# Projections and self attention of a two-layer transformer kernel, joined in one program for each engine

## The chip, the cores and the metric

One core of a Trainium2 chip. The engines are TensorE (PE; PEld is its weight load), VectorE (DVE), ScalarE (ACT), GpSimd (POOL) and SyncE (SP), which here only issues DMAs. The metric is the device time of one execution in microseconds.

## The reference, cut to what matters

Two layers over x of shape (4, 1024, 256), each cross attention and then a feed-forward part. The change is in the first layer's feed-forward part, which begins with a self attention of 16 heads of 16:

```
src = layernorm(x)
q = (src @ q_w).reshape(b, s, h, hd).transpose(0, 2, 1, 3)
k = (src @ k_w).reshape(b, s, h, hd).transpose(0, 2, 1, 3)
v = (src @ v_w).reshape(b, s, h, hd).transpose(0, 2, 1, 3)
scores = jnp.einsum('bhqd,bhkd->bhqk', q, k) / np.float32(np.sqrt(hd))
scale = jax.nn.sigmoid(jnp.einsum('bhsd,hd->bhs', q, scale_w)) * 2.0
aw = jax.nn.softmax(scores * scale[..., None], axis=-1)
out = jnp.einsum('bhqk,bhkd->bhqd', aw, v).transpose(0, 2, 1, 3).reshape(b, s, d)
```

## The kernel before

`self_projections` runs over 8 chunks of 512 tokens (a batch is two chunks). For a chunk c, DVE normalizes x (`layernorm`, `ln_apply`), PE transposes the result and ACT copies it to `srcT`; PE then computes v (`vps`, L817), q (`qps`, L825) and k (`kps`, L832), transposes the next chunk (L807), and multiplies q by the scale weights (`zps`, L841). q and k are split into three bf16 parts each: ACT makes the first (`kpart[..., 0]`), DVE the rest (`krest`, L706), ACT the second part (L781), POOL the third (L736). For q, ACT's tanh of `zps` (`th`, L787) and a product on DVE (`qT`, L710) come first, then the same steps (L791, L715, L793, L740). SP stores all parts to DRAM (`q_parts`, `k_parts`, `v_groups`). The middle batches are a hardware loop. At the end SP waits for the last store, the block ends on all engines, and semaphores are cleared.

`self_attention` is a second block. It takes 16 groups of 4 heads, each loaded from DRAM into one of three sets of `qs`, `ks`, `vs`. A unit is a group and one half (512) of its queries; there are 32 units. A unit has 8 key tiles of 128. Scores are made transposed (keys on partitions), so the maximum over keys has to be known before: it is taken one or two units ahead from another product. A pair of matmuls (`first_scores`, L1106, in a buffer of `aps`) gives 128 queries by 512 keys of two heads, and DVE reduces it (`maximum`, L1020); a unit needs 16 of these pairs. `combine` joins them, PE transposes the maxima (`transpose_max`, L1118), ACT negates them (`keep_max`, L1064), POOL splits them (`split_max`) and SP passes them through DRAM (`pass_max`) into two rows of `qs`. In the main loop, every key tile has four `scores` (L1137) in three rotating buffers `bps`, one for each head, whose exponentials ACT writes to `ex` (L1086), and one `weigh_values` (8 matmul records, L1147) into `ops`. Two of the pairs for units ahead stand in each key tile. The order on PE is: a score, two pairs, a score, the weighing of the key tile before, two scores. The weighing waits for that tile's last exponential. Once in a unit ACT copies `ops` out (`keep_out`, L1056) and PE transposes it (L1127).

Before the main loop the 16 pairs of unit 0 and the first 12 of unit 1 are made with nothing beside them.

Of the kernel before, what the change touches and what calls it, by code (L numbers as in the profile page):

```python
# [13 lines left out]
P = 128  # L14
# [573 lines left out]
def self_projections(nc, x_sb, src_sb, ident, eps_pow, w, q_parts, k_parts, v_dram):  # L588

    with ExitStack() as ctx:  # L590
        kit = Kit(nc, ctx, "sp_")
        sb, ps, sem = kit.sb, kit.ps, kit.sem
        turnstile = sem("turnstile")
        wts = sb("wts", [P, 3, HALVES, D])
        swcol = sb("swcol", [P, HALVES])
        swblk = sb("swblk", [P, HALVES, P])
        stats, mv = sb("stats", [P, CT, 6]), sb("mv", [P, CT, 2])
        var, rstd = sb("var", [P, CT]), sb("rstd", [P, CT])
        xn = sb("xn", [P, CT, D])
# [2070 lines left out]
```

## Time and profile before

| | us |
|---|---|
| median of three runs | 2056.4 (2055.46 to 2056.41) |
| the profiled execution's own time | 2058.98 |
| its span, first to last instruction | 2056.9 |
| SP's first DMA of the projections | 248.9 |
| DVE's first statistics of the projections | 254.4 |
| first transpose, first v projection on PE | 259.2, 262.3 |
| first pair for the maxima | 392.4 |
| first exponential | 425.1 |
| last exponential | 1124.8 |

The stage in question is the stretch from 248 to 1133 us; what comes ahead and behind is not touched by the diff. In a timeline row, the first number is the start, the second the time until the end of the last of the merged instructions, and the brackets name what ended the idle time before it.

### The profile page before, as it was taken

To read this page: it belongs to the slowest core of one execution; us is meant where nothing else is said; L and a number is where in the kernel's file an instruction comes from. 1 tells how busy PE (TensorE), PEld (TensorE's weight loads), DVE (VectorE), ACT (ScalarE), POOL (GpSimd) and SP (SyncE) were. 2 spreads that over 40 slices of the span, in tenths; PEclk is the share of its full clock that TensorE was granted. 3 is DMA by queue.
4 is the path that set the end of the run, shared out by engine and by line. 5 is a ranking of instruction groups with operands and counts; after the bars stand their busy time and mean duration, and the time that the engine had idled before them with its cause. 6 is when DMAs were issued, how large, how long until landed. Compare 5 with 4: busy or idle time off the path is not lost. (4 is left out here: it accounts for less than half of the span.)

```text
span 2056.9 us, 30275 instructions
## 1 busy us (share of the span) xinstructions
PE 1713.4 (83%) x10579; PEld 808.6 (39%) x10580; DVE 1250.0 (61%) x2123; ACT 969.1 (47%) x1811; POOL 603.5 (29%) x645
## 2 busy tenths in 40 slices
PE   5799799389999999999997884999077996329997
PEld 3466455012222222222221563776044663125654
DVE  5344344588888888888881484665783554562221
ACT  3422256158888888888887331444242332102110
POOL 4300034613222122121122264666561001120533
PEclk9899989679999999999999995999588998758998
DMA  5000048711221111321100622221400003310542
GB/s 138 1 2 1 16 156 288 208 38 38 55 56 38 38 38 38 67 45 37 38 2 1 220 80 85 59 69 56 125 1 1 1 1 124 135 32 11 124 122 31
DMA packets 112675, 134.48 MB, mean 65 GB/s; under 512 B 18481, under 2 KB 88497, under 8 KB 112273
## 3 DMA queue, kind: packets, MB, share of 16 engines
q1 hardware_dynamic: 101824, 114.20, 20.5%
q0 software_dynamic: 9552, 17.83, 3.6%
q8 instruction: 86, 1.41, 0.3%
q10 hardware_dynamic: 1152, 0.54, 0.1%
q14 instruction: 61, 0.49, 0.1%
HBM read 78.47 MB, written 53.93 MB: 64 GB/s over the span
## 5 line engine op out<-in xcount | busy, mean ns | idle before, releaser
L1020 DVE TENSOR_REDUCE sa_mhalf<-sa_a 128x2 f32<-128x1024 f32 x512 | 602.3, 1221 | 86.8 <-PE sa_a L1106 86.8
L1086 ACT ACTIVATE sa_e<-sa_b 128x512 f32<-128x512 f32 x1024 | 534.5, 601 | 139.4 <-PE sa_b L1137 139.4
L1137 PE MATMUL sa_b<-sa_q,sa_k 112*128 112x512 bf16 x1024 | 311.1, 385 | 3.2 <-ACT sa_e L1086 3.0
L1147 PE MATMUL sa_ops<-sa_e,sa_v 128*17 128x512 f32 x2048 | 270.4, 599 | 6.3 <-ACT sa_e L1086 1.1
L1137 PEld LDWEIGHTS sa_b<-sa_q,sa_k 112*128 112x128 bf16 x1024 | 78.8, 97 | 322.6 <-ACT sa_e L1086 281.6
L1106 PE MATMUL sa_a<-sa_k,sa_q 48*128 48x512 bf16 x1024 | 168.2, 398 | 38.4 <-DMA sa_k<-k_parts 24.5
L993 POOL TENSOR_TENSOR sa_rden<-sa_o_rows,sa_minus_one 128x16 f32<-128x16 f32 x32 | 93.1, 2908 | 180.1 <-ACT sa_o_rows L1072 180.1
L213 DVE TENSOR_REDUCE xa_mx<-xa_rows 128x16 f32<-128x1024 f32 x64 | 78.3, 1224 | 102.6 <-PE xa_rows L445 102.6
L982 POOL CAST sa_negm<-sa_neg 16x128 bf16<-16x128 f32 x32 | 9.0, 281 | 380.1 <-issue 338.0
L1106 PEld LDWEIGHTS sa_a<-sa_k,sa_q 48*128 48x128 bf16 x1024 | 42.1, 93 | 177.6 <-issue 77.0
L360 ACT ACTIVATE xa_pT<-xa_cols 128x1024 f32<-128x1024 f32 x64 | 62.1, 1021 | 84.9 <-PE xa_cols L477 84.9
L2552 DVE TENSOR_TENSOR sw_hT<-sw_p,sw_act 128x512 f32<-128x512 f32 x32 | 22.1, 692 | 101.9 <-PE sw_p L2497 101.9
L2465 POOL DMA_INDIRECT out_x<-sw_yo,tc_idx x32 | 49.9, 1560 | 105.5 <-DVE sw_yo L2559 98.5
L1637 PE MATMUL ex_hps<-at_w,ex_xT 128*128 x156 | 77.3, 619 | 1.9 <-ACT ex_xT L1677 1.9
L445 PE MATMUL xa_rows<-xa_kblk,xa_qT 64*128 64x256 f32 x512 | 73.1, 407 | 6.1 <-DVE xa_mx L213 5.3
L2541 ACT ACTIVATE sw_act<-sw_p 128x512 f32<-128x512 f32 x32 | 19.1, 597 | 118.8 <-PE sw_p L2491 110.3
L1660 PE MATMUL ex_yps<-at_attn,ex_hT 128*128 x312 | 74.1, 380 | 0.5 <-ACT ex_hT L1687 0.4
L544 PE MATMUL xa_cols<-c_ctxT,c_wts 128*128 128x256 f32 x16 | 7.5, 652 | 78.0 <-PEq L43 64.5
L1687 ACT ACTIVATE ex_hT<-ex_tps,at_bt,at_g 128x128 f32<-128x128 f32 x156 | 58.8, 457 | 15.7 <-PE ex_tps L1648 15.7
L726 POOL TENSOR_TENSOR sp_var<-sp_mv,x_eps_pow 128x4 f32<-128x4 f32 x8 | 7.5, 939 | 190.7 <-DVE sp_mv L683 190.7
L2491 PE MATMUL sw_p<-sw_xT,tc_w 128*128 128x512 f32 x128 | 62.0, 608 | 1.2 <-ACT sw_xT L2530 1.2
L1147 PEld LDWEIGHTS sa_ops<-sa_e,sa_v 128*17 128x17 f32 x2048 | 34.9, 95 | 69.5 <-ACT sa_e L1086 48.8
(328 smaller groups left out, 2819.7 us busy)
## 6 DMA issues: line engine op xcount, KB each, us to landing
k_parts<-sp_kpart SPq DMA_DIRECT2D x96, 128.0 KB, 1.8
sa_q<-q_parts SPq DMA_DIRECT2D x64, 192.0 KB, 5.1
sa_k<-k_parts SPq DMA_DIRECT2D x64, 192.0 KB, 5.6
tc_w<-in_L_ffn_W SPq DMA_DIRECT2D x24, 512.0 KB
q_parts<-sp_qpart SPq DMA_DIRECT2D x16, 384.0 KB, 3.3
ex_xg<-expert_in SPq DMA_DIRECT2D x39, 132.0 KB
v_groups<-sp_vt SPq DMA_DIRECT2D x8, 544.0 KB, 4.1
sa_v<-v_groups SPq DMA_DIRECT2D x16, 272.0 KB, 7.3
```

The lines of the kernel that those rows point to most:

```text
L213: nc.vector.tensor_reduce(mx[:, t], rows[:].rearrange("p r (n k) -> p (r n) k", k=SC), axis=X, op=ALU.max).then_inc(max_done, 1)
L360: nc.scalar.activation(pT[:, 4 * half + 2 * part:4 * half + 2 * part + 2], cols[:, 2 * part:2 * part + 2], ACT.Exp, scale=SCALE).then_inc( ...
L445: last = nc.tensor.matmul(rows[:, r, half * D:(half + 1) * D], qT[part, half, tokens], kblk[part, c // 2, half, CT * r:CT * (r + 1)], star ...
L993: nc.gpsimd.tensor_tensor(rden[:], view[:, :, :, DK], minus_one[:], ALU.pow).then_inc(rden_made, 1)
L1020: nc.vector.tensor_reduce(mhalf[a % 2][:, half, head:head + PAIRED + 1:PAIRED, t], aps[use % 2][:], axis=X, op=ALU.max).then_inc(a_used, 1)
L1086: nc.scalar.activation(ex[kt % 2][:, head], bps[use % 3][:], ACT.Exp, scale=SCALE).then_inc(b_used, 1)
L1106: last = nc.tensor.matmul(aps[use % 2][:, h // PAIRED], qs[s][rows, h, q0:q0 + P], ks[s][rows, h, half * CW:(half + 1) * CW], start=True, ...
L1137: nc.tensor.matmul(bps[use % 3][:], ks[s][:, head, kt * P:(kt + 1) * P], qs[s][:, head, qc * CW:(qc + 1) * CW], start=True, stop=True).the ...
L1147: last = nc.tensor.matmul(ops[32 * head:32 * head + VW], vs[s][:, kt, head], ex[kt % 2][:, head], start=(kt == 0), stop=(kt == KT - 1))
L1637: last = nc.tensor.matmul(hps[j % 2][:], xT[j % 2][:, half], ew["w1"][:, half, ds(e, 1), :], start=(half == 0), stop=(half == HALVES - 1))
L1660: last = nc.tensor.matmul(yps[j % 2][:, 0:D], hT[j % 2][:, f], ew["w2"][:, f, ds(e, 1), :], start=(f == 0), stop=(f == FK - 1))
L2491: last = nc.tensor.matmul(p1[f % 2][:], w1[e % 3][:, half, f * P:(f + 1) * P], xT[e % 2][:, half], start=(half == 0), stop=(half == HALVES ...
```

## The change

Both functions become one, with one program per engine. What changes in it:

- SP no longer waits for all stores and there is no block end in the middle. Sets 0 and 1 are loaded in chunks 2 and 4, among the stores. Set 2 lies in the memory of the bf16 parts, so POOL zeroes its idle rows and SP loads it after all parts are stored, in unit 0.
- In chunks 4 to 7, six pairs of matmuls a chunk are placed between the projections (`early_scores`), and six reductions among DVE's steps. These are the 16 of unit 0 and 8 of unit 1; four more follow the last chunk. All 24 use one buffer, `aps[1]`, since `aps[0]` holds `vps`. The maxima of unit 0 are transposed in chunk 7 and passed on among the last stores.
- `zps` shares the memory of `qps`: the q projection of a chunk waits for the `th` of the chunk before.
- The copy of the normalized rows on ACT (L750, `keep_src`) is gone: DVE writes `src_sb` itself. The first layernorm no longer stands behind the wait for the weights.
- `ex` has three buffers, and the weighing runs two key tiles behind (LAG = 2). `keep_out` moves from the second to the sixth exponential of a unit. The buffers share memory with `srcT`, `wts`, `qT`, `th`, `qrest` and `krest`.
- The chunk loop is written out; the semaphores of both parts are cleared after the attention.

```diff
+    FIRST_EARLY, EARLY_CHUNKS = CHUNKS // 2, CHUNKS // 2
+    PER_CHUNK = 6
+    PROJECTION_USES = PER_CHUNK * EARLY_CHUNKS
+    LAG = 2
+    def a_slot(use):
+        return 1 if use < PROJECTION_USES else use % 2
+    def a_before(use):
+        if use == PROJECTION_USES:
+            return None
+        return use - 1 if use < PROJECTION_USES else use - 2
+        vps, kps, qps = aps[0], ps("b01", [P, HALVES, CW]), ps("b2o", [P, HALVES, CW])
+        bps, ops = [kps[:, 0], kps[:, 1], qps[:, 0]], qps[:, 1]
+        def early(c, j):
+            return None if c < FIRST_EARLY else divmod(PER_CHUNK * (c - FIRST_EARLY) + j, TILE_MAXIMA)
...
+                for c in range(CHUNKS):
+                    store_v(c)
+                    if c == 2:
+                        load(0, 0, True)
+                    if c == 4:
+                        load(1, 1, True)
+                    store_k(c)
+                    if c == CHUNKS - 2:
+                        pass_max(0, 0, 0)
+                    store_q(c)
...
+                for c in range(CHUNKS):
+                    if c >= 1:
+                        scale_q(c - 1)
+                    early_maximum(c, 0)
+                    if c >= 1:
+                        rest_q(c - 1)
+                    early_maximum(c, 1)
+                    if c + 1 < CHUNKS:
+                        normalize_x(c + 1)
+                    early_maximum(c, 2)
+                    if c + 2 < CHUNKS:
+                        layernorm(c + 2)
...
+                    early_maximum(c, 3)
+                    early_maximum(c, 4)
+                    rest_k(c)
+                    early_maximum(c, 5)
+                scale_q(CHUNKS - 1)
+                nc.vector.memset(ops, 0.0).then_inc(out_cleared, 1)
+                rest = range(PROJECTION_USES - TILE_MAXIMA, EARLY)
+                for k in rest[0:2]:
+                    maximum(1, k)
+                rest_q(CHUNKS - 1)
+                for k in rest[2:]:
+                    maximum(1, k)
...
-                            if head == 0 and n >= 1 or kt >= 2 and head == 0:
-                                act.wait_ge(pv_done, KT * n + kt - 1)
+                            if i == LAG * GH and n == 0:
+                                act.wait_ge(k3, CHUNKS)
+                                act.wait_ge(q3, CHUNKS)
+                            if head == 0 and KT * n + kt > LAG:
+                                act.wait_ge(pv_done, KT * n + kt - LAG)
...
-                            if i == 1 and n >= 1:
+                            if i == GH + 1 and n >= 1:
                                 keep_out(n)
...
-                            if kt:
-                                weigh_values(n, kt - 1, s, turn)
+                            if kt >= LAG:
+                                weigh_values(n, kt - LAG, s, turn)
```

On PE, in the middle of the projections before: a chunk's v, q and k projections, the next chunk's transposes, the scale product (names begin with `sp_`).

```order
L817 MATMUL sp_vps<-sp_wts,sp_srcT 128x256 x8
L825 MATMUL sp_qps<-sp_srcT,sp_wts 128x512 x4
L832 MATMUL sp_kps<-sp_srcT,sp_wts 128x512 x4
L807 MATMUL sp_vps<-x_ident,sp_xn 128x128 x8
L841 MATMUL sp_zps<-sp_qT,sp_swblk 128x512 x2
```

On PE in chunk 5 of the changed kernel. `sa_a0` is `vps`, `sa_b2o` is `qps`, `sa_b01` is `kps`, `sa_e0` holds `srcT` and the weights; L1104 is a pair for the maxima, in `sa_a1`.

```order
L1203 MATMUL sa_a0<-sa_e0 128x256 x4
L1104 MATMUL sa_a1<-sa_k0,sa_q0 128x512 x2
L1203 MATMUL sa_a0<-sa_e0 128x256 x4
L1104 MATMUL sa_a1<-sa_k0,sa_q0 128x512 x2
L1194 MATMUL sa_b2o<-sa_e0 128x512 x4
L1104 MATMUL sa_a1<-sa_k0,sa_q0 128x512 x2
L1194 MATMUL sa_b01<-sa_e0 128x512 x2
L1104 MATMUL sa_a1<-sa_k0,sa_q0 128x512 x2
L1194 MATMUL sa_b01<-sa_e0 128x512 x2
L1104 MATMUL sa_a1<-sa_k0,sa_q0 128x512 x2
L1183 MATMUL sa_a0<-x_ident,sm_src 128x128 x8
L1104 MATMUL sa_a1<-sa_k0,sa_q0 128x512 x2
```

The projections are the same matmuls; six pairs now stand between them.

On DVE, one chunk of the middle before (chunk 1): the split of k, the scaled q, the split of q, the next normalization.

```order
L706 TENSOR_TENSOR sp_krest<-sp_kps,sp_kpart 128x1024
L710 SCALAR_TENSOR_TENSOR sp_qT<-sp_th,sp_qT 128x1024
L715 TENSOR_TENSOR sp_qrest<-sp_qT,sp_qpart 128x1024
L693 TENSOR_SCALAR sp_xn<-x_x,sp_mv,sp_rstd 128x256 x4
L677 BN_STATS sp_stats<-x_x 128x6 x4
L683 BN_AGGR sp_mv<-sp_stats 128x2 x4
```

On DVE in the changed kernel, from the `rest_k` of chunk 4 (L933) to that of chunk 5; L938 and L945 are the scaled and split q, L892 is a reduction.

```order
L933 TENSOR_TENSOR sa_e<-sa_b,sa_parts 128x1024
L892 TENSOR_REDUCE sa_mhalf<-sa_a 128x2
L938 SCALAR_TENSOR_TENSOR sa_e<-sa_e 128x1024
L892 TENSOR_REDUCE sa_mhalf<-sa_a 128x2
L945 TENSOR_TENSOR sa_e<-sa_e,sa_parts 128x1024
L892 TENSOR_REDUCE sa_mhalf<-sa_a 128x2
L926 TENSOR_SCALAR sm_src<-x_x,sp_mv,sp_rstd 128x256 x4
L892 TENSOR_REDUCE sa_mhalf<-sa_a 128x2
L914 BN_STATS sp_stats<-x_x 128x6 x4
L920 BN_AGGR sp_mv<-sp_stats 128x2 x4
L892 TENSOR_REDUCE sa_mhalf<-sa_a 128x2 x2
L933 TENSOR_TENSOR sa_e<-sa_b,sa_parts 128x1024
```

Six reductions came in, one between nearly every two steps.

## Rows read from the trace of the kernel before

**Rows 1.** The page: busy time, and one line of its DMA issues.

```profile
PE 1713.4 (83%) x10579; PEld 808.6 (39%) x10580; DVE 1250.0 (61%) x2123; ACT 969.1 (47%) x1811; POOL 603.5 (29%) x645
...
sa_k<-k_parts SPq DMA_DIRECT2D x64, 192.0 KB, 5.6
```

**Rows 2.** Stretches: busy us of each engine, granted clock, DMA share, GB/s.

```profile
82.00:92.00 10.00, 7.08 (x32) 4.80 (x31) 2.90 (x4) 0.60 (x1) 0.00 (x0) 0.50 0.01 2
220.00:230.00 10.00, 8.25 (x128) 5.00 (x124) 2.40 (x3) 3.51 (x5) 0.00 (x0) 1.00 0.01 2
304.00:317.00 13.00, 13.00 (x46) 7.69 (x45) 6.88 (x16) 9.08 (x13) 6.42 (x4) 1.00 0.84 281
393.00:425.00 32.00, 16.82 (x58) 2.83 (x54) 30.88 (x29) 0.27 (x1) 19.20 (x13) 0.50 0.77 150
```

**Rows 3.** Timeline, the entry into the projections.

```profile
253.83 0.49 DVE L668 TENSOR_TENSOR sp_swblk<-x_headmask,sp_swcol 128x128 f32<-128x128 f32 x2 [6.12 <-DMA sp_swcol<-in_L_ffn_scale_w]
254.40 0.37 DVE L677 BATCH_NORM_STATS2 sp_stats<-x_x 128x6 f32<-128x256 f32 x1
262.26 6.67 PE L817 MATMUL sp_vps<-sp_wts,sp_srcT 128*128 128x256 f32 x16 [1.11 <-ACT sp_srcT L756]
```

**Rows 4.** Timeline, one middle chunk.

```profile
278.23 3.62 PE L817 MATMUL sp_vps<-sp_wts,sp_srcT 128*128 128x256 f32 x16
291.15 3.62 PE L817 MATMUL sp_vps<-sp_wts,sp_srcT 128*128 128x256 f32 x16
289.81 1.23 DVE L706 TENSOR_TENSOR sp_krest<-sp_kps,sp_kpart 128x1024 f32<-128x1024 f32 x1 [1.72 <-ACT sp_kpart L777]
291.07 1.06 ACT L781 ACTIVATE sp_kpart<-sp_krest 128x1024 bf16<-128x1024 f32 x1 [0.38 <-DVE sp_krest L706]
292.20 2.13 POOL L736 TENSOR_TENSOR sp_kpart<-sp_krest,sp_kpart 128x1024 bf16<-128x1024 f32 x1 [4.05 <-ACT sp_kpart L781]
294.02 1.40 DVE L710 SCALAR_TENSOR_TENSOR sp_qT<-sp_th,sp_qT 128x1024 f32<-128x1024 f32 x1 [2.98 <-ACT sp_th L787]
```

**Rows 5.** Timeline, the end of the projections to the first exponential.

```profile
366.03 1.88 PE L841 MATMUL sp_zps<-sp_qT,sp_swblk 128*128 128x512 f32 x4
369.68 2.12 POOL L736 TENSOR_TENSOR sp_kpart<-sp_krest,sp_kpart 128x1024 bf16<-128x1024 f32 x1 [4.04 <-ACT sp_kpart L781]
370.55 2.33 DVE L710 SCALAR_TENSOR_TENSOR sp_qT<-sp_th,sp_qT 128x1024 f32<-128x1024 f32 x1 [2.04 <-ACT sp_th L787]
392.42 1.03 PE L1106 MATMUL sa_a<-sa_k,sa_q 48*128 48x512 bf16 x4 [24.51 <-DMA sa_k<-k_parts]
393.07 18.20 DVE L1020 TENSOR_REDUCE sa_mhalf<-sa_a 128x2 f32<-128x1024 f32 x16 [1.12 <-PE sa_a L1106]
425.14 0.60 ACT L1086 ACTIVATE sa_e<-sa_b 128x512 f32<-128x512 f32 x1 [12.87 <-PE sa_b L1137]
```

**Rows 6.** Timeline, PE and ACT around a unit's second key tile, and a later tile.

```profile
713.27 2.06 ACT L1086 ACTIVATE sa_e<-sa_b 128x512 f32<-128x512 f32 x4
713.40 0.64 PE L1106 MATMUL sa_a<-sa_k,sa_q 48*128 48x512 bf16 x4
713.97 0.39 PE L1137 MATMUL sa_b<-sa_q,sa_k 112*128 112x512 bf16 x1
714.50 1.05 PE L1147 MATMUL sa_ops<-sa_e,sa_v 128*17 128x512 f32 x8
719.65 0.39 PE L1137 MATMUL sa_b<-sa_q,sa_k 112*128 112x512 bf16 x1
719.97 1.05 PE L1147 MATMUL sa_ops<-sa_e,sa_v 128*17 128x512 f32 x8
```

**Rows 7.** Timeline, a key tile of the last unit, without pairs.

```profile
1108.65 2.07 ACT L1086 ACTIVATE sa_e<-sa_b 128x512 f32<-128x512 f32 x4 [0.58 <-PE sa_b L1137]
1109.78 1.05 PE L1147 MATMUL sa_ops<-sa_e,sa_v 128*17 128x512 f32 x8
1111.20 2.07 ACT L1086 ACTIVATE sa_e<-sa_b 128x512 f32<-128x512 f32 x4 [0.48 <-PE sa_b L1137]
```

More of the change, by code:

```diff
@@ L1038, in body @@
                                     maximum(*ahead(n, kt, which))
-                nc.vector.memset(o_sb[:], 1.0).then_inc(out_cleared, 1)
-                nc.vector.memset(ops[:], 0.0).then_inc(out_cleared, 1)
-                for i, (tile, (rows, heads)) in enumerate((tile, idle) for tile in (qs[0], ks[0]) for idle in IDLE):
-                    nc.vector.memset(tile[rows, heads], 0.0).then_inc(idle_zeroed, 1)
-                for k in range(TILE_MAXIMA):
-                    maximum(0, k)
-                combine(0)
@@ new lines, in early_maximum, with make_swblk @@
+                def early_maximum(c, j):
+                    if early(c, j):
+                        maximum(*early(c, j))
+                        if (c - FIRST_EARLY, j) == MAX_MADE:
+                            combine(0)
+                def make_swblk():
+                    dve.wait_ge(loaded, 32)
+                    for half in range(HALVES):
+                        nc.vector.tensor_tensor(swblk[:, half].rearrange("p (h d) -> p h d", d=DK),
+                                                bc(w["headmask"][:], 2, [P, HH, DK]),
+                                                bc(swcol[:, half:half + 1].broadcast_to([P, HH]), 2, [P, HH, DK]),
+                                                ALU.mult).then_inc(blk_made, 1)
@@ L1055, in keep_out @@
                     act.wait_ge(pv_done, KT * n)
[L1056 removed]
+                    nc.scalar.activation(o_sb[:], ops, ACT.Copy).then_inc(o_evacuated, 1)
                 def keep_max(a):
@@ L1090, in _ @@
+                evacuate_srcT(0)
+                for c in range(CHUNKS):
+                    chunk(c)
                 act.wait_ge(out_cleared, 2)
-                keep_max(0)
                 groups(body)
@@ new lines, in early_scores, with project @@
+                def early_scores(c, j):
+                    if early(c, j):
+                        a, k = early(c, j)
+                        first_scores(a, k, 0, 0, a)
+                def project(out, f, half):
+                    for k in range(HALVES):
+                        last = nc.tensor.matmul(out[:, half], wts[:, f, k, half * P:(half + 1) * P], srcT[:, k],
+                                                start=(k == 0), stop=(k == HALVES - 1))
+                    return last
```

530 lines of the change are left out of this document (260 added, 270 removed).

## The prediction

> **What bounds the kernel now.** I read the page, then the busy time by stretches, then the timeline around the seams. TensorE is the busiest engine, 83% of the span [rows 1], but a busy share says little here; the question is what each stretch waits for. The projections run at TensorE's pace: from one v projection to the next are 291.15 - 278.23 = 12.92 us, with TensorE busy for all of 13.00 [rows 2, 4]. DVE has 6.88 us of work in them. After the last product, at 367.9, nothing feeds TensorE for 24.5 us: the last parts are made and stored, the block ends, set 0 is loaded [rows 5]. Then VectorE sets the pace: 30.88 of 32 us busy, 16 reductions in 18.20 us (1.14 apart), TensorE at a granted clock of 0.50, which is 1.2 GHz [rows 2, 5]. ACT has its first exponential at 425.14. From the product's end to there are 57 us in which the two big stages don't overlap. In the main loop TensorE goes from key tile to key tile, and the weighing also waits for ACT at some places [rows 6, 7].
>
> **The entry.** DVE has stood idle from 247.71 to 253.83 for the weights [rows 3]. In the changed kernel its statistics stand ahead of that wait. SP's first DMA at 248.9 shows when the block is open, so statistics move from 254.40 to about 248.9: 5.5 us. The v projection still needs the weights, which are there by 253.8; it comes at 262.26 - 5.5 = 256.8. Bounds: 0 and 6.7 us. Chunk 0 to chunk 1 stays 15.97 us, so chunk 4 begins at 256.8 + 15.97 + 3 x 12.92 = 311.5.
>
> **Chunks 4 to 7.** A matmul of 512 columns is 0.21 us at 2.4 GHz. From a score to the weighing behind it are 0.32 us [rows 6], so a change of the tile's shape costs about 0.11. A pair inside the projections then costs 0.21 + 2 x 0.11 = 0.43, six of them 2.6: by TensorE alone a chunk would be 15.5 us. VectorE gets 6 x 1.14 = 6.8 us on top of 6.9, and its order now matters, since one buffer makes pair and reduction alternate. I walk one chunk from the start of `rest_k`, t = 0:
> - `rest_k` 1.23, ACT's second part 1.06 [rows 4], POOL's third part 2.13: until 4.5. The scaled q can't end before POOL is done: in the middle chunk it took 1.40 us and ended 1.1 after POOL; in the last chunk it took 2.33, from 370.55, and again ended 1.1 after POOL's 371.80 [rows 4, 5]. So 5.6.
> - A reduction of 1.2: 6.9. TensorE stood before its pair: 7.35. The q projection takes 3.4 (as v's 3.62 less the tail), the third pair and its tail 0.65: 11.4.
> - Reduction 12.6, layernorm 1.9 (four statistics at 0.37 [rows 3], the aggregates as an estimate 0.4): 14.5, the fourth reduction 15.7. Only now the fifth pair may be filled, 0.65, and its reduction ends at 17.7, where the next `rest_k` begins.
>
> That is 17.7 us for chunk 5. Without a layernorm TensorE's order is the longer path: 7.35 + 6.8 for q and k + 3 x 0.45 + 0.2 + a reduction 1.2 = 16.9 for chunks 6 and 7. From chunk 4's v projection to its `rest_k` was 11.6 (289.81 - 278.23), now with four pairs (1.7) and the same queue behind layernorm (3.2) 16.5. After the last `rest_k`: scaled q 5.6, the clearing of `ops` 0.5, two reductions 2.3, `rest_q` 1.23 and ACT's part 1.06, with handovers 10.8. ACT takes them in order, so the first exponential is at 311.5 + 16.5 + 17.7 + 2 x 16.9 + 10.8 = 390.3, against 425.1: **34.8 us** earlier. If everything ran at TensorE's 15.5, this would be 40; with 1 us lost at each pair's wait, 24 pairs, less than 20.
>
> The Trainium skill, page SBUF — State Buffer, section Who interferes with whom, says that a DVE instruction with two SBUF inputs waits for a GpSimd one that reads SBUF. The trace agrees: the two L710 rows, 1.40 and 2.33. A plan by 1.1 us for that step regardless of POOL would give chunks 0.9 shorter and some 3.5 us less in all.
>
> **The start of the main loop.** TensorE has little to do between its last product and the first exponential, some 8 us, so I expect half clock there again; before, the first key tiles ran so, too. The first two key tiles now have no weighing: 0.5 us gained. Were the clock full, it would be 3.5.
>
> **The later weighing.** At a unit's second tile ACT copies `ops` out first, so the four exponentials begin at 713.27; the second one's end, 714.39, releases the weighing at 714.50, 0.53 behind its score at 713.97. Where ACT is ahead it comes 0.32 behind (719.65 to 719.97) [rows 6]. With two tiles of distance these 0.21 us go in 30 units: **6.3**. The other tiles show 0.32, which is TensorE's own order, so nothing is gained there. Where no pairs are left, 14 key tiles at the end, the chain is exponential, exponential, weighing, score: 1111.20 - 1108.65 = 2.55 [rows 7]. With the later weighing it goes over the three buffers: an exponential 0.60 and a handover, the score to weighing 0.32, the weighing 0.99, score to exponential 0.43, in all 2.38. 14 x 0.17 = **2.4**. Bounds for both together: 0, and 14 x (2.55 - 2.07) + 30 x 0.42, twice the wait, = 19.
>
> **What I cost at nothing, and its cover.** ACT's copy (L750) goes, but DVE waits for POOL, not for ACT. The q projection now waits for `th`; that ends at about 294.0 and the projection began when v's 3.4 us were over, at 294.6, so 0.6 us cover it, 1.6 with ACT's copy gone; past that it is paid eight times. The loads of sets 0 and 1 are 18 DMAs on SP ahead of k stores. The DMA engines are at 0.84 of a chunk's 13 us [rows 2], so 2.1 us are free in each; a set takes at most 0.77 x 32 / 3 = 8.2. Stores of chunk 2 then land about 6 us late, and their buffers are written again 20 us later. Set 0 is issued near 302, lands in 5.6 us [rows 1], and the first pair is due at 313: 5 us of cover. POOL's memsets for set 2, six of 1.8 us, fit into unit 0 between two maxima, 21 us apart; behind them stand only the bias of x and the next maximum. One more clearing of semaphores stands at the end: 0 to 1.1 us, I take 0.8, because it stood in the seam before.
>
> **The sum.** 34.8 + 0.5 + 6.3 + 2.4 - 0.8 = 43.2 us. Against the profiled execution, 2058.98 (span 2056.9 and 2.1 around it), this is 2015.8; the median of the runs is 2.6 below that execution, so 2056.4 - 43.2 = **2013.2**.
>
> **The rivals.**
> - *The later weighing brings nothing* (0.20). The 0.21 us is taken up by DVE: its two reductions, 1.14 + 1.22, fill 2.36 of a tile's 2.6. Then 2013.2 + 8.7 = 2022.
> - *The joined chunks run at TensorE's pace* (0.13). For it: DVE has only some 14 us of work in a chunk. Against it: the single buffer and POOL's hold. Then chunk sums fall by 2.2 + 1.4 + 1.4 and the lead by 1: 2007.
> - *The joined chunks are dearer* (0.12): set 0 lands after 313, the backlog of stores delays ACT, or waits on TensorE cost more than 0.45 a pair. 5 to 15 us: 2018 to 2028, 2024 in the middle.
> - *The main loop's tiles shrink everywhere* (0.04). Were the 0.32 a hidden wait, DVE's 2.36 would be the next bound: 240 tiles x 0.1 = 24 us more, 1989.
> - *Slower* (0.03): the granted clock falls to half through chunks 4 to 7. From 82 to 92 us TensorE was busy for 7.08 of 10 us and had 0.50. The chunks' 15.5 us of TensorE work would take 31 instead of about 17.5: 4 x 13.5 = 54 us, 2067. It decides from about three whole chunks on. Against it: at 8.25 of 10 us busy, 220 to 230 us, the clock was 1.00 [rows 2], and a joined chunk has 15.5 of 17.5. The Trainium skill, TensorE: Matmul & The Clock Gate, section A second HAM failure mode, says that short idle gaps between groups, when PSUM buffers cycle, can make the clock go back and forth; by that rule this case is real, and the 82 to 92 row agrees that it happens.
> - *The overlap is not had* (0.02): the pairs cost among the projections what they cost alone, 33 us, and only the seam goes: 2036.
>
> **How the numbers follow.** The forecast has 0.46, with its own range 2008 to 2018. From the rivals above, 2004 to 2026 leaves out the shrunk tiles, the slow case, the unhad overlap, and the tails of the dearer chunks and of TensorE's pace: near 0.2. A measurement of this kernel tells about 0.2% (4 us) from no change. Faster 0.96, same 0.01, slower 0.03.
>
> **What the changed profile would show.** The first v projection near 256.8; chunks 0 to 3 still 12.9 apart; v projections of chunks 5 to 7 some 17 to 19 us apart, DVE waiting for PE's pairs and PE for reductions; L938 ending 1.1 us after POOL's part; the first exponential near 390 at half clock; key tiles still 2.60, the unit's second weighing 0.32 behind its score, units 0.2 shorter; 2.4 in the last unit. Wrong would be: chunks at 20 or more, a DMA as releaser of a pair in chunk 4, half clock inside the chunks.

## The result, and the profile after

The changed kernel takes 2010.67 us (median of 4 runs, 2008.15 to 2014.48), the kernel before on the same chip 2055.93 (4 runs): ratio 0.9784, 95% interval 0.9769 to 0.9798. A second comparison on another chip gave 0.9778 (0.9758 to 0.9798), 2011.38 against 2057.24. The forecast was 2013.2 and a gain of 43.2 us; the medians are 45.3 us apart.

The profiled execution took 2008.15 us, 50.8 less than the one before (2058.98). Not all of that is the change. The last product of cross attention, which nobody touched, starts 3.83 us earlier in the profile of after, and behind the changed stage there are 920.5 us instead of 923.5. So I count inside the stage, from VectorE's last copy ahead of it (L236, at 247.02 before, 243.19 after) to the next stage's first transposes (L1492 at 1133.43 before, L1552 at 1085.90 after): 886.41 us before, 842.71 after, **43.7 us less**. To compare a moment of after with one of before, add 3.83 to it. The two ends of that stretch in the timeline of before, which weren't shown yet, and then of after:

```profile
247.02 0.69 DVE L236 TENSOR_TENSOR x_x<-xa_front,x_x 128x512 f32<-128x512 f32 x1 [0.96 <-PE xa_front L514]
...
1133.43 1.09 PE L1492 MATMUL ao_tps<-x_ident,at_attn 128*128 128x128 f32 x4 [5.54 <-PEq L43]
```

```profile
243.19 0.69 DVE L236 TENSOR_TENSOR x_x<-xa_front,x_x 128x512 f32<-128x512 f32 x1 [0.96 <-PE xa_front L514]
...
1085.90 1.09 PE L1552 MATMUL ao_tps<-x_ident,at_attn 128*128 128x128 f32 x4 [5.82 <-PEq L43]
```

The page of after, busy time: TensorE's work is about the same in a shorter span.

```profile
PE 1703.1 (85%) x10580; PEld 805.3 (40%) x10580; DVE 1256.7 (63%) x2123; ACT 962.7 (48%) x1803; POOL 598.9 (30%) x645
```

The timeline of after at the entry, answering to [rows 3].

```profile
245.06 1.41 DVE L914 BATCH_NORM_STATS2 sp_stats<-x_x 128x6 f32<-128x256 f32 x4 [1.18 <-PEq L43]
251.04 0.46 DVE L956 TENSOR_TENSOR sp_swblk<-x_headmask,sp_swcol 128x128 f32<-128x128 f32 x2
252.77 6.07 PE L1203 MATMUL sa_a<-sa_e 128*128 128x256 f32 x16 [1.21 <-ACT sa_e L1045]
```

The statistics come 1.9 us behind VectorE's copy, with no DMA as releaser; `swblk` is made later and holds nobody. From the copy to the first v projection are 9.58 us; before they were 15.24. The 16 matmuls of that projection take 6.07 us, where they took 6.67 [rows 3].

The timeline of after in chunk 5, from one `rest_k` (L933) to the next, VectorE, POOL and TensorE's pairs (rows between left out). The last row is the `rest_k` behind it.

```profile
323.25 1.22 DVE L933 TENSOR_TENSOR sa_e<-sa_b,sa_parts 128x1024 f32<-128x1024 f32 x1
...
325.69 2.13 POOL L862 TENSOR_TENSOR sa_parts<-sa_e,sa_parts 128x1024 bf16<-128x1024 f32 x1 [3.76 <-ACT sa_parts L1070]
...
326.79 2.12 DVE L938 SCALAR_TENSOR_TENSOR sa_e<-sa_e 128x1024 f32<-128x1024 f32 x1 [1.19 <-ACT sa_e L1074]
...
330.10 0.39 PE L1104 MATMUL sa_a<-sa_k,sa_q 48*128 48x512 bf16 x2 [0.43 <-DVE sa_mhalf L892]
...
332.30 3.18 DVE L926 TENSOR_SCALAR sm_src<-x_x,sp_mv,sp_rstd 128x256 f32<-128x256 f32 x4
332.48 2.21 POOL L867 TENSOR_TENSOR sa_parts<-sa_e,sa_parts 128x1024 bf16<-128x1024 f32 x1 [4.66 <-ACT sa_parts L1082]
...
335.41 1.21 DVE L892 TENSOR_REDUCE sa_mhalf<-sa_a 128x2 f32<-128x1024 f32 x1
336.54 1.39 DVE L914 BATCH_NORM_STATS2 sp_stats<-x_x 128x6 f32<-128x256 f32 x4
...
338.13 1.19 DVE L892 TENSOR_REDUCE sa_mhalf<-sa_a 128x2 f32<-128x1024 f32 x1
...
339.38 0.39 PE L1104 MATMUL sa_a<-sa_k,sa_q 48*128 48x512 bf16 x2 [0.40 <-DVE sa_mhalf L892]
...
339.81 1.23 DVE L892 TENSOR_REDUCE sa_mhalf<-sa_a 128x2 f32<-128x1024 f32 x1 [0.49 <-PE sa_a L1104]
...
340.95 1.22 DVE L933 TENSOR_TENSOR sa_e<-sa_b,sa_parts 128x1024 f32<-128x1024 f32 x1
```

The chunk lasts 17.70 us. The scaled q ends 1.09 us behind POOL's part, as the walk had it. The normalization (L926) takes 3.18 us where its four pieces took 1.4 before, beside POOL's third part of q: that isn't in the walk. The releaser of each waiting pair is a reduction, never a DMA.

The end of the projections and the first exponential, to be read against [rows 5].

```profile
375.05 1.22 DVE L933 TENSOR_TENSOR sa_e<-sa_b,sa_parts 128x1024 f32<-128x1024 f32 x1
...
382.42 0.61 PE L1104 MATMUL sa_a<-sa_k,sa_q 48*128 48x512 bf16 x2 [4.38 <-DVE sa_mhalf L892]
...
385.61 0.58 ACT L1037 ACTIVATE sa_e<-sa_b 128x512 f32<-128x512 f32 x1
```

On the scale of before the first exponential is at 389.44 instead of 425.14. A pair that took 0.39 in chunk 5 takes 0.61 at 382.42: TensorE stood still for 4.38 us and came back at half clock. The window rows (busy us of each engine, granted clock, DMA share, GB/s) say the same, and that the clock never fell inside the joined chunks, which the first row spans.

```profile
308.00:376.00 68.00, 61.33 (x210) 29.02 (x209) 57.21 (x64) 31.37 (x43) 20.75 (x14) 1.00 0.93 293
326.00:343.00 17.00, 15.54 (x55) 7.44 (x54) 15.72 (x21) 7.83 (x11) 5.24 (x4) 1.00 1.05 258
380.00:385.00 5.00, 1.76 (x5) 0.31 (x5) 4.89 (x6) 1.41 (x2) 0.00 (x0) 0.55 0.70 241
385.00:390.00 5.00, 3.67 (x12) 0.73 (x12) 4.17 (x5) 3.07 (x6) 2.12 (x1) 0.50 0.43 144
```

In the main loop, a score, the weighing behind it, and a key tile without pairs, answering to [rows 6, 7].

```profile
717.54 0.39 PE L1137 MATMUL sa_b<-sa_q,sa_k 112*128 112x512 bf16 x1
717.86 1.05 PE L1147 MATMUL sa_b2o<-sa_e,sa_v 128*17 128x512 f32 x8
...
1056.28 0.39 PE L1137 MATMUL sa_b2o<-sa_q,sa_k 112*128 112x512 bf16 x1
...
1058.66 0.60 PE L1137 MATMUL sa_b<-sa_q,sa_k 112*128 112x512 bf16 x2
```

The weighing at 717.86 belongs to a unit's second key tile and comes 0.32 us behind its score, where it was 0.53. Without pairs a key tile lasts 2.38.

### The profile page after: what moved, and what is told of

Its sections match the earlier page's. It is cut to its first block and busy times, and to the rows that moved or that the text cites. A ratio compares the mean times of both kernels' runs of the same rounds, so it can differ in the third digit from the quotient of the medians.

```text
span 2006.4 us, 30050 instructions
## 1 busy us (share of the span) xinstructions
PE 1703.1 (85%) x10580; PEld 805.3 (40%) x10580; DVE 1256.7 (63%) x2123; ACT 962.7 (48%) x1803; POOL 598.9 (30%) x645
## 5 line engine op out<-in xcount | busy, mean ns | idle before, releaser
L892 DVE TENSOR_REDUCE sa_mhalf<-sa_a 128x2 f32<-128x1024 f32 x512 | 604.3, 1221 | 84.4 <-PE sa_a L1104 82.7
L1037 ACT ACTIVATE sa_e<-sa_b 128x512 f32<-128x512 f32 x683 | 383.4, 601 | 76.9 <-PE sa_b L1137 76.9
L1147 PE MATMUL sa_b2o<-sa_e,sa_v 128*17 128x512 f32 x2048 | 269.7, 598 | 0.0
L1037 ACT ACTIVATE sa_e<-sa_b2o 128x512 f32<-128x512 f32 x341 | 205.0, 601 | 40.6 <-PE sa_b2o L1137 40.6
L1137 PE MATMUL sa_b<-sa_q,sa_k 112*128 112x512 bf16 x468 | 163.4, 388 | 2.7 <-ACT sa_e L1037 2.7
L1104 PE MATMUL sa_a<-sa_k,sa_q 48*128 48x512 bf16 x704 | 113.3, 389 | 13.2 <-DVE sa_mhalf L892 13.2
L1137 PEld LDWEIGHTS sa_b<-sa_q,sa_k 112*128 112x128 bf16 x468 | 40.6, 97 | 151.2 <-ACT sa_e L1037 134.4
L1137 PE MATMUL sa_b2o<-sa_q,sa_k 112*128 112x512 bf16 x236 | 91.3, 387 | 0.6 <-ACT sa_e L1037 0.5
L1104 PEld LDWEIGHTS sa_a<-sa_k,sa_q 48*128 48x128 bf16 x704 | 30.5, 93 | 114.7 <-issue 56.7
L1137 PE MATMUL sa_b<-sa_parts 112*128 112x512 bf16 x215 | 73.5, 384 | 0.0
```

Of the source, the lines that this page charges most:

```text
L892: nc.vector.tensor_reduce(mhalf[a % 2][:, half, head:head + PAIRED + 1:PAIRED, t], aps[a_slot(use)][:], axis=X, op=ALU.max).then_inc(a_use ...
L1037: nc.scalar.activation(ex[(KT * n + kt) % (LAG + 1)][:, head], bps[use % 3], ACT.Exp, scale=SCALE).then_inc(b_used, 1)
L1104: last = nc.tensor.matmul(aps[a_slot(use)][:, h // PAIRED], qs[s][rows, h, q0:q0 + P], ks[s][rows, h, half * CW:(half + 1) * CW], start=Tr ...
L1137: nc.tensor.matmul(bps[use % 3], ks[s][:, head, kt * P:(kt + 1) * P], qs[s][:, head, qc * CW:(qc + 1) * CW], start=True, stop=True).then_i ...
L1147: last = nc.tensor.matmul(ops[32 * head:32 * head + VW], vs[s][:, kt, head], ex[(KT * n + kt) % (LAG + 1)][:, head], start=(kt == 0), stop ...
```

## The experiments

Times of different chips can't be set side by side (the kernel before took 2043.29 us on one, 2057.24 on another, and the traces put that into stages that nobody changed), so each run's ratio is to the kernel before on its own chip, and what is small is read inside the trace. "Chunks" are the distances between the v projections of chunks 4 and 5, 5 and 6, 6 and 7; "lead" goes from the last of them to the first exponential; "loop" from the first to the last exponential (all in us).

| kernel | ratio to before (95%) | chunks | lead | loop |
|---|---|---|---|---|
| before | 1 | 12.91, 12.92, 12.91 | 69.4 | 699.7 |
| after | 0.9784 (0.9769 to 0.9798) | 18.66, 17.71, 17.24 | 25.1 | 691.4 |
| after_again | 0.9778 (0.9758 to 0.9798) | 18.66, 17.71, 17.24 | 25.1 | 691.3 |
| before_entry | 0.9970 (0.9956 to 0.9984) | 12.91, 12.91, 12.91 | 70.0 | 699.1 |
| before_lag2 | 0.9956 (0.9942 to 0.9970) | 12.91, 12.91, 12.91 | 69.5 | 690.7 |
| lag1 | 0.9804 (0.9789 to 0.9818) | 18.66, 17.71, 17.24 | 25.1 | 700.6 |
| noearly | 0.9837 (0.9825 to 0.9850) | 12.91, 12.91, 13.50 | 51.1 | 690.8 |
| norm_first | 0.9769 (0.9749 to 0.9789) | 17.80, 16.85, 16.85 | 25.1 | 690.9 |
| dve_order | 0.9763 (0.9741 to 0.9784) | 17.96, 17.00, 16.85 | 25.1 | 692.2 |
| short_k3 | 0.9747 (0.9726 to 0.9768) | 17.49, 16.81, 16.36 | 23.8 | 690.8 |
| stats_early | 0.9763 (0.9740 to 0.9787) | 17.81, 16.85, 16.85 | 25.1 | 692.4 |
| warm_tail | 0.9750 (0.9726 to 0.9773) | 17.81, 16.84, 16.85 | 25.2 | 690.9 |
| warm_tail2 | 0.9775 (0.9758 to 0.9792) | 17.81, 16.85, 16.85 | 25.2 | 692.3 |

**The entry alone: before_entry.** The kernel before; `blocks` is the making of `swblk` with its wait for the weights.

```diff
-                dve.wait_ge(loaded, 32)
...
                 layernorm(0)
                 ln_apply(0)
                 layernorm(1)
+                blocks()
...
+                transpose_xn(0)
                 pe.wait_ge(loaded, 32)
                 pe.wait_ge(blk_made, 4)
-                transpose_xn(0)
```

> The kernel before with only the first two tiles' layernorm and transposes put ahead of the wait for the projections' weights. Theory (the prediction's entry term): the first V projection starts 5.5 us earlier and the whole stage with it, so 5 to 6 us faster, 2050 to 2051. Rival (the weights' transfer ends last there anyway, and the earlier layernorm only waits at another place): within 1 us of the kernel before.

Measured: 5.1 us between the medians (2038.20 against 2043.29), ratio 0.9970. In its trace, from the copy L236 to the first v projection:

```profile
249.34 0.69 DVE L236 TENSOR_TENSOR x_x<-xa_front,x_x 128x512 f32<-128x512 f32 x1 [0.96 <-PE xa_front L514]
...
257.89 0.46 DVE L669 TENSOR_TENSOR sp_swblk<-x_headmask,sp_swcol 128x128 f32<-128x128 f32 x2
...
259.26 4.18 PE L819 MATMUL sp_vps<-sp_wts,sp_srcT 128*128 128x256 f32 x9 [1.21 <-ACT sp_srcT L758]
```

9.92 us instead of 15.24, so 5.3 us come from this edit alone; and chunk 0 lasts 15.21 us instead of 15.97, 0.8 more. The lead is 0.5 us longer and the loop 0.5 shorter than before, so that these two cancel. The theory holds and the rival falls.

**The later weighing, taken out and put in alone: lag1 and before_lag2.** The diff is that of lag1; before_lag2 puts the same into the kernel before.

```diff
-    LAG = 2
+    LAG = 1
...
-                            if i == GH + 1 and n >= 1:
+                            if i == GH * (LAG - 1) + 1 and n >= 1:
                                 keep_out(n)
```

> The changed kernel with the weighing of the values back at one key tile behind its scores (LAG = 1, two exponential buffers); all else as changed. Theory (the prediction's main-loop term): each unit's second key tile waits again for the reciprocal behind the exponentials, some 0.21 us in each of 30 units, and the last 14 key tiles of the stage lose their 0.17 us each: 6.3 + 2.4 = 8.7 us; the two profiles gave 8.3. So 7 to 9 us slower than the changed kernel, 2018 to 2020, and the first exponential where it is in the changed kernel. Rival (the later weighing brings nothing, and the shorter main loop comes of the joined program): within 1 us of the changed kernel, about 2011.

> The kernel before with only the later weighing (LAG = 2, a third exponential buffer), its programs apart as before. Theory (the main-loop term stands alone and needs nothing of the joined program): 7 to 9 us faster than the kernel before, 2047 to 2049. Rival (it pays only together with the joined program, or not at all): within 1 us of the kernel before.

Measured: before_lag2 is 9.8 us below the kernel before by the medians, and 9.0 in the loop (690.7 against 699.7). lag1's loop is 9.2 us longer than that of after (700.6 against 691.4), with the first exponential as far behind the last v projection as in after. lag1's whole time doesn't show it as clearly: its ratio, 0.9804, is 0.0020 to 0.0026 above that of after, 4 to 5 us where 7 to 9 were expected, and the intervals overlap (its five runs spread from 2001.39 to 2008.90). In lag1's trace the old wait is back: a unit's second score and its weighing are 0.53 us apart.

```profile
720.82 0.39 PE L1137 MATMUL sa_b2o<-sa_q,sa_k 112*128 112x512 bf16 x1
721.35 1.05 PE L1147 MATMUL sa_b2o<-sa_e,sa_v 128*17 128x512 f32 x8
```

The units, read as distances between ACT's copies of the transposed result (L1072 before, L1020 after), are 21.84 us with one tile of distance and 21.635 with two: 0.21 in each, the size in the sum. The last three distances fall from 21.61, 21.07 and 10.18 to 21.26, 19.81 and 9.85. The gain belongs to the later weighing and needs nothing of the joined program.

**The joined program without the early pairs: noearly.** All 28 early pairs behind chunk 7, with the combining, transposing and split of the first maximum behind them.

```diff
-            return None if c < FIRST_EARLY else divmod(PER_CHUNK * (c - FIRST_EARLY) + j, TILE_MAXIMA)
+            return None
...
-    PROJECTION_USES = PER_CHUNK * EARLY_CHUNKS
+    PROJECTION_USES = 0
...
-                for k in range(PROJECTION_USES - TILE_MAXIMA, EARLY):
+                for k in range(TILE_MAXIMA):
+                    first_scores(0, k, 0, 0, 0)
+                pe.wait_ge(krest_made, CHUNKS)
+                transpose_max(0)
+                for k in range(EARLY):
                     first_scores(1, k, 0, 0, 1)
```

> The changed kernel without the pairs of early maxima among the projections: all 28 pairs come after chunk 7, with the combining and the split of the first maximum behind them; the rest as changed. Theory (the seam and the overlap are two gains): chunks 5 to 7 fall from 17.2 to 18.7 us to 12.9 each (some 14.9 us less from the V projection of chunk 4 to that of chunk 7), and the 21 pairs that then stand alone cost about 25 us behind it, so that the first exponential comes 9 to 13 us later than in the changed kernel, best value 10.7, time about 2021. Rival 1 (the overlap brings nothing, since the pairs only stretch the chunks by what they take alone): within 2 us of the changed kernel. Rival 2 (the overlap is the whole gain of the seam): over 25 us slower, above 2036.

Measured: 0.9837, by which it is 11 to 12 us slower than the changed kernel (0.9784, 0.9778); in the traces the first exponential comes 90.4 us behind chunk 4's v projection, against 78.7 in after and 108.2 before. So of 29.4 us the joined program with its early load of set 0 brings 17.8, and the pairs inside the chunks another 11.7. Both rivals fall. What the pairs cost where they stand alone is seen in VectorE's group of reductions between 361 and 400 us, and in the row of that stretch:

```profile
L890 DVE TENSOR_REDUCE sa_mhalf<-sa_a 128x2 f32<-128x1024 f32 x28 | 31.9, 1211 | 1.1 <-PE sa_a L1103 1.1
...
361.00:400.00 39.00, 17.32 (x61) 3.05 (x60) 35.72 (x33) 4.39 (x6) 4.94 (x4) 0.57 0.54 185
```

28 reductions take 31.9 us with only 1.1 us of waiting, so VectorE is the bound. TensorE runs at little more than half clock on the mean, and VectorE hardly waits for it.

**VectorE's order in a chunk: norm_first and dve_order.** Beside them after_again, the changed kernel unaltered, on the same chip. norm_first changes the place of one step:

```diff
-                    early_maximum(c, 1)
                     if c + 1 < CHUNKS:
                         normalize_x(c + 1)
+                    early_maximum(c, 1)
                     early_maximum(c, 2)
                     if c + 2 < CHUNKS:
                         layernorm(c + 2)
```

dve_order has the last two steps the other way round besides: `layernorm(c + 2)`, then `early_maximum(c, 2)`.

> The changed kernel once more, unaltered, beside the three variants below, so that they are compared on one chip. Expected: the v projections of chunks 4 to 7 again 18.66, 17.71 and 17.24 us apart, the main loop from first to last exponential again 691 us, and the ratio to the kernel before again 0.977 to 0.980.

> The changed kernel with VectorE's normalization of the next tile ahead of the second early maximum instead of behind it, so that it no longer lies beside POOL's third part of q. Theory (the normalization is held by POOL, 3.18 us instead of 1.38, and lies on the chunk's path): chunks 5 and 6 shorter by 0.7 to 0.9 us each and the lead to chunk 5 too, some 2 us less in all; the four normalizations back at 1.4 us. Rival (that hold is hidden behind the q projection's matmuls, since the next pair is filled only behind them): the v projections stay 18.7, 17.7 and 17.2 us apart and the time is the same within 0.5 us.

> The changed kernel with VectorE's order in a chunk changed at two places: normalization, second maximum, layernorm statistics, third maximum. Theory (VectorE's order with one buffer for the pairs sets the pace of chunks 5 and 6, as the walk of the prediction has it, so the statistics belong where TensorE has its long q projection): the chunks with a layernorm fall to TensorE's order, 16.9 to 17.1 us, some 2 us less in all than the changed kernel. Rival (TensorE's order binds already): the same within 0.5 us. Second rival (the third pair is now filled too late and TensorE waits for the reduction behind the statistics): chunks longer by up to 1.8 us.

Measured: after_again repeats the chunks of after to 0.01 us. In norm_first they are 0.86, 0.86 and 0.39 us shorter, 2.1 in all, with the normalization back at its own duration: the group L926 between 306 and 378 us, first of after, then of norm_first (busy us, mean ns).

```profile
L926 DVE TENSOR_SCALAR sm_src<-x_x,sp_mv,sp_rstd 128x256 f32<-128x256 f32 x12 | 9.6, 856 | 0.0
```

```profile
L926 DVE TENSOR_SCALAR sm_src<-x_x,sp_mv,sp_rstd 128x256 f32<-128x256 f32 x12 | 4.1, 408 | 0.0
```

So the hold of the normalization was on the path. dve_order gains 1.8: its chunks 4 and 5, the two with statistics, are 0.15 us longer than those of norm_first, so the statistics are better left behind the third maximum. norm_first's median is 2008.18 against 2011.38 for after_again, and its ratio 0.9769 against 0.9778: the whole times agree with 2.1 us but can't prove it, and they can't rank the two orders either (0.9769 and 0.9763).

**The statistics ahead of the scaled q: stats_early.** On norm_first:

```diff
+                    apart = FIRST_EARLY <= c < CHUNKS - 2
+                    if apart:
+                        statistics(c + 2)
                     if c >= 1:
                         scale_q(c - 1)
...
-                        layernorm(c + 2)
+                        layernorm(c + 2, apart)
```

> The kernel of norm_first, and in chunks 4 and 5 VectorE's four statistics stand ahead of the scaled q instead of behind the third maximum, in a gap of 1.19 us in which VectorE waits for ACT; there they lie partly beside POOL's third part of k. Theory (the gap takes them, since the scaled q can't end before POOL's part in any case): chunk 4 falls from 17.80 us to TensorE's own 16.85, chunk 5 stays 16.85, 0.9 us less than norm_first in all. Rival (statistics are held by POOL as the normalization was, 1.4 us becoming up to 3): the scaled q ends 1 to 1.6 us later and chunks 4 and 5 are that much longer.

Measured: 17.81 and 16.85, exactly norm_first. The theory falls: the statistics weren't what makes chunk 4 longer by 0.96. The rival falls too, as the trace of stats_early shows.

```profile
328.29 1.39 DVE L916 BATCH_NORM_STATS2 sp_stats<-x_x 128x6 f32<-128x256 f32 x4
328.48 2.13 POOL L862 TENSOR_TENSOR sa_parts<-sa_e,sa_parts 128x1024 bf16<-128x1024 f32 x1 [5.12 <-ACT sa_parts L1079]
329.61 2.08 DVE L944 SCALAR_TENSOR_TENSOR sa_e<-sa_e 128x1024 f32<-128x1024 f32 x1
```

Four statistics take their 1.39 us right beside POOL's part, and the scaled q behind them still ends 1.08 us after it.

The traces show where the 0.96 lies. Measured from `rest_k` to `rest_k`, chunk 4 isn't longer: in norm_first these steps are 16.86, 16.84, 16.86 and 16.84 us from chunk 3 to chunk 7 (16.85 on the mean), and in after the first is 17.72, as chunk 5's 17.70. What differs is where the v projection stands in the step. It begins 1.34 us behind chunk 3's `rest_k` and 2.28 us behind chunk 4's (306.87 - 305.53 and 325.53 - 323.25 in after), since chunk 3 has no pairs at its end and chunk 4 has two. So in chunk 4 TensorE is early and waits for the reduction behind the scaled q: its second pair in after waits 1.38 us, where chunk 5's waits 0.43.

```profile
312.39 0.39 PE L1104 MATMUL sa_a<-sa_k,sa_q 48*128 48x512 bf16 x2 [1.38 <-DVE sa_mhalf L892]
```

There was nothing in chunk 4 for the earlier statistics to win.

**Without POOL's hold on the scaled q: short_k3.** It leaves out nearly all of k's third part from chunk 2 on, so it is a measurement and no version to use.

```diff
+                    if c < 2:
+                        nc.gpsimd.tensor_tensor(kpart[c % 2][:, 2], krest, kpart[c % 2][:, 1], ALU.subtract).then_inc(k3, 1)
+                    else:
+                        nc.gpsimd.tensor_tensor(kpart[c % 2][:, 2, :, 0:8], krest[:, :, 0:8], kpart[c % 2][:, 1, :, 0:8], ALU.subtract).then_inc(k3, 1)
```

> The changed kernel with POOL's third part of k made for only 16 of 1024 columns from chunk 2 on (work left out: the third part of k is stale there). Theory (POOL's 2.13 us hold the scaled q, and that hold is on the chunk's path): the scaled q takes 1.15 to 1.4 us instead of 2.12, and chunks 5 to 7 and the tail behind the last chunk lose 0.7 to 1.0 us each, 3 to 4 us in all, as the prediction puts it for a plan without POOL's hold. Rival (the hold is covered, since the pair behind it waits for TensorE's v projection): chunks unchanged, at most 1 us less, in the tail alone.

Measured: the chunks lose 1.17, 0.90 and 0.88 us, the lead 1.4, in all 4.3. The medians on one chip, 2004.67 against 2011.38, are 6.7 apart; the trace has these 4.3 up to the first exponential and 0.6 in the loop. POOL's part takes 0.22 us and the scaled q 1.23:

```profile
341.66 0.22 POOL L865 TENSOR_TENSOR sa_parts<-sa_e,sa_parts 128x16 bf16<-128x16 f32 x1 [3.76 <-ACT sa_parts L1073]
342.75 1.23 DVE L941 SCALAR_TENSOR_TENSOR sa_e<-sa_e 128x1024 f32<-128x1024 f32 x1 [1.19 <-ACT sa_e L1077]
```

The hold is on the path in every chunk and behind the last one, as the walk had it.

**Keeping TensorE's clock up in the tail: warm_tail and warm_tail2.** On norm_first; `again` writes a pair so many times more.

```diff
-                    first_scores(1, k, 0, 0, 1)
+                    first_scores(1, k, 0, 0, 1, {9: 10, 10: 1, 11: 2}.get(k, 0))
```

warm_tail2 has `{9: 20, 10: 1, 11: 2}`.

> The kernel of norm_first, and in the tail behind the last chunk TensorE writes three of its four pairs of early scores several times over (11, 2 and 3 times; the same numbers into the same place, and only the last write is announced), so that it has no pause of 4.4 us ahead of the first scores. Theory (TensorE falls to a granted clock of 0.50 there because it stands still, and the first key tiles pay for it): the clock stays 1.00 from 360 to 400 us on the profile's scale; the first exponential comes at most 0.5 us earlier, since ACT's chain sets it, but the first four key tiles run at 2.6 us each, and from the first to the last exponential there are 2.0 to 3.5 us less than the 690.9 of norm_first. Rival (the first key tiles are slow for another reason, their loads or VectorE's maxima): the same 690.9 within 0.5 us. Second rival (the repeated writes hold up the reductions): the first exponential up to 2 us later.

> The kernel of warm_tail with the second pair of the tail written 21 times instead of 11. In warm_tail the 24 matmuls took only 2.77 us, TensorE still stood idle for 2.23 us, and the clock had fallen by the next pair. Now the writes last 4.8 to 5.0 us, to the moment when the next pair may be written. Theory (the pause makes the clock fall): the clock stays 1.00 over the tail, the first exponential comes within 0.5 us of where it was (25.1 us behind the v projection of chunk 7), and from the first to the last exponential there are 2.0 to 3.5 us less than 690.9. Rival (the clock falls there whatever TensorE does, or the first key tiles are slow for another reason): 690.9 within 0.5 us again.

Measured: in warm_tail 24 matmuls took 2.77 us, a pause of 2.23 stayed, the clock fell all the same, and the loop is 690.9. In warm_tail2 the pause ahead of the next pair is 0.65 us, and the stretches read:

```profile
375.00:380.00 5.00, 4.44 (x28) 1.80 (x30) 3.81 (x4) 2.08 (x2) 2.13 (x1) 1.00 0.69 234
380.00:385.00 5.00, 4.28 (x37) 1.46 (x33) 4.87 (x5) 1.06 (x1) 0.00 (x0) 1.00 0.64 221
385.00:390.00 5.00, 3.36 (x11) 0.73 (x12) 4.65 (x5) 2.92 (x5) 2.12 (x1) 0.63 0.38 129
390.00:395.00 5.00, 5.00 (x21) 0.85 (x17) 4.25 (x5) 3.36 (x7) 0.00 (x0) 0.50 0.82 279
```

The clock now holds over the tail and falls 3.1 us later against the first exponential, when TensorE waits for VectorE's reductions in pauses of 1.12 and 0.52 us among the first key tiles. That these pauses are the cause of the second fall was not tested. The half-clock stretch was moved into the key tiles: it runs from 0.2 to 10.5 us behind the first exponential, in norm_first from 2.9 ahead of it to 7.3 behind, 10.2 us both times; from the first exponential to ACT's first copy of a result (`o_rows`) are 38.7 us against 37.4, and that is all by which the loop grew (690.9 to 692.3). So the clock fell in the tail where TensorE paused and held where the pause was filled, and half clock in the first key tiles costs about 0.4 us per us (1.3 / 3.2). The expectation that full clock in the tail shortens the loop by 2.0 to 3.5 us failed. By the 0.4, full clock in all the first key tiles would give some 3 us (7.3 x 0.4), an estimate, since no run had it, and likely too high: in short_k3 the half clock ends 1.4 us earlier than in norm_first, 6.0 us behind the first exponential, and the first copy comes only 0.3 us earlier (37.05), which is 0.24 per us.

The same reading explains why kernels with one and the same main loop differ in the table by 1.5 us, 690.8 to 692.4. The units are equal to 0.01 us; what differs is where the half clock ends: 7.2 to 7.3 us behind the first exponential in noearly, norm_first and warm_tail, 8.4 to 8.5 in after, after_again and lag1, 10.2 to 10.5 in dve_order, stats_early and warm_tail2. short_k3 is the exception: 6.0 us and yet 690.8. Its first copy is 0.3 us earlier, as said, but each of its units is some 0.006 us longer, which takes 0.2 back.

## Why the prediction was right, step by step

- **The entry** (5.5 us forecast): 5.66, and 5.3 alone in before_entry. The forecast held chunk 0 at 15.97 us; it took 15.36, 0.6 more gained. All of it lies in the v projection, 6.67 us before and 6.07 after: its first part runs at a granted clock of 0.50, which ends 6.0 us behind the projection's start before and 4.8 after. In before_entry it ends 4.5 us behind, and chunk 0 takes 15.21.
- **Chunks 4 to 7.** From chunk 4's v projection to the first exponential the forecast had 78.8 us, the trace has 78.74. Inside, the steps between the `rest_k` are 17.70, 17.25 and 16.85 where 17.7, 16.9 and 16.9 stood; the lead to the first is 16.38 (16.5), and from the last to the first exponential 10.56 (10.8). But **one step of the walk failed**: "Without a layernorm TensorE's order is the longer path". The layernorm isn't what makes chunk 5 longer. In norm_first chunk 5 has it and lasts 16.85, as the chunks without it, so there the path is the one that the walk gave to chunks 6 and 7: the held scaled q, a reduction, then TensorE's order. What made 17.70 was the normalization, held by POOL for 3.18 us instead of 1.38. The walk had given the hold to the scaled q alone and left the normalization at no cost. The third reduction therefore ended 13.4 us behind `rest_k` (335.41 + 1.21 - 323.25) and not 12.6. The walk made up for it: its layernorm of 1.9 us took 1.6 (336.54 to 338.13), its 0.65 for the fifth pair was a wait of 0.49, and its last step, 15.7 + 0.65 + 1.2, gives 17.55 where 17.7 was written. The 17.7 was right because errors cancelled. In chunk 6, which has a normalization and no layernorm, they didn't: 17.25 against 16.9.
- **POOL's hold on the scaled q.** The Trainium skill, SBUF — State Buffer, section Who interferes with whom, was cited for it, and the forecast priced a plan without it at 0.9 us a chunk and 3.5 in all. short_k3 measured 0.9 to 1.2 a chunk and 4.3 in all, and the scaled q at 1.23 us without the hold agrees with what the page says. The same section counts tensor_scalar, the form of the normalization, among the instructions that can contend with GpSimd, namely in modes that use both ports; I didn't ask that of the normalization. Which mode it ran in no run shows.
- **The seam and the overlap** stood in the sum as one term, 34.8; from the copy L236 to the first exponential it is 35.7. noearly parts it: 17.8 for the joined program, 11.7 for the pairs inside the chunks, and 6.3 for the entry and the shorter chunk 0. So the rival "the overlap is not had", at 2036, was priced too high: noearly is 1.6% faster than before, which is 33 us.
- **The start of the main loop** (0.5 forecast) was mis-sized. From the first exponential to ACT's first copy of a result are 39.15 us in lag1 and 37.85 in after, with the half clock ending at the same place, so the later weighing gains 1.3 in this unit. Against the kernel before (38.31, its half clock ending 7.0 us behind the first exponential) only 0.5 is left, because the half clock now lasts 1.5 us longer into the key tiles: in before_lag2, where it ends at 7.0 too, the same distance is 37.08, and the gain 1.2. The 0.5 came out by chance.
- **The later weighing** (6.3 + 2.4): 28 units are 0.21 shorter, 5.8 us, and the last three distances give 0.35 + 1.26 + 0.33 = 1.9. With the first unit's 1.2 to 1.3 that is 9.0, as lag1 and before_lag2 have it; in after, with the clock's 0.7 or so taken off, the loop is 8.3 shorter. The 30 units of 6.3 were 28, and the end gave 1.9 for 2.4. The rival that it brings nothing is excluded, and so is the one in which all key tiles shrink, since a unit of eight tiles shrank by no more than its 0.21.
- **The clearing of semaphores** (0.8): from the last exponential to the next stage are 8.9 us instead of 8.6, so 0.3, and it was mis-sized.
- **The sum:** 35.7 + 8.3 - 0.3 = 43.7 against 43.2. The medians' 45.3 hold 1.6 us more, which is less than their runs differ by.
- **The half clock in the chunks**, the slower rival: granted 1.00 from 326 to 343 with TensorE busy for 15.54 of 17 us. The Trainium skill, TensorE: Matmul & The Clock Gate, section A second HAM failure mode, was the rule that spoke for it. The waits ahead of chunk 5's pairs are 0.30 to 0.43 us, the longest in the joined chunks 1.38, and the granted clock stayed 1.00: no run here shows such a fall inside the chunks. In the tail behind the last chunk it did fall, as forecast.
- **The two rivals about the chunks** (all at TensorE's own pace, or 5 to 15 us dearer) both fall, since the stretch from chunk 4's v projection to the first exponential came within 0.1 us of the forecast.
- **The cover** for set 0's load held: the first pair, at 308.69, doesn't wait for a DMA.

What stays open: what the first key tiles would give at full clock, and what makes the clock fall there in warm_tail2. Of the versions that leave nothing out and repeat nothing, norm_first is the best by its trace: from chunk 4's v projection to the first exponential it takes 2.1 us less than the changed kernel.

## What to carry to other kernels

When two stages are joined, walk one period of the slowest shared buffer over all engines, with every instruction of the queue in it, and ask of each one that reads SBUF what lies beside it on POOL: the hold may fall on a step that had been free, as it fell on the normalization here. A right total is no proof of its parts; a change of order that costs nothing, like norm_first's one moved line, tests them. A wait of 0.2 us that repeats in every unit is worth a third buffer: it gave 9 us here by itself, with no other part of the change.

## What the runs showed of the hardware

- Beside POOL's 2.2 us of tensor_tensor, VectorE's TENSOR_SCALAR on 128x256 with two operands per partition took 3.18 us for four instead of 1.38 (after against norm_first). Four BATCH_NORM_STATS2 of the same shape beside POOL took 1.39, as alone (stats_early). So the hold depended on the form of the instruction.
- Pairs of 48-row matmuls of 512 columns in different row groups, written one behind the other without a wait, took 2.77 us for 24 (warm_tail), 0.115 each; the projections' 128-row f32 matmuls of 512 columns took 0.45 to 0.46 each (eight in 3.60 us before, 3.70 in after).
- Filling TensorE's pause with repeated matmuls moved the half-clock stretch and didn't shorten it: 10.2 us in norm_first, warm_tail and warm_tail2, the last one 3.1 us later against the first exponential.
- The same stretch lasted 13.6 to 13.7 us in after, after_again, lag1, dve_order and stats_early and 10.2 in norm_first. Where it ended decided the cost: the distance from the first exponential to the first copy of a result went from 37.4 us (end at 7.3, norm_first) over 37.85 (8.5, after) to 38.7 (10.5, stats_early and warm_tail2), so that kernels with equal units differed in the loop by up to 1.5 us.
- At the entry the same: the v projection of chunk 0 took 6.67 us with half clock for its first 6.0 us (before) and 6.07 with half clock for 4.8 (after).
